# Graph network and mixture layers on one core: the last columns of the dense attention by heads, one-hots shared out by thirds, and the end of the edge layer

## The reference, cut to what matters

```python
e = jax.nn.leaky_relu(el[src] + er[dst], NEG_SLOPE)
m = jax.ops.segment_max(e, dst, num_segments=N)
ex = jnp.exp(e - m[dst])
den = jax.ops.segment_sum(ex, dst, num_segments=N)
out = jax.ops.segment_sum((ex / den[dst])[:, :, None] * feat[src], dst, num_segments=N)
```

```python
sigma = jax.nn.sigmoid(out_src[src] + out_dst[dst])
h = Uh + segment_sum(Vh[src] * sigma, dst) / (segment_sum(sigma, dst) + 1e-06)
x = x + relu(layernorm(h) * gamma + beta)
H = gelu(layernorm(x) @ W1 + b1)
probs = softmax(H @ Wg + bg); assign = argmax(probs)
out = x + probs[assign] * (H @ Wd[assign] + bd[assign])
```

## Time and profile before

| | before |
|---|---|
| median of 3 runs | 3075.07 us (3072.62 to 3076.36) |
| the profiled execution | 3073.93 us, span 3072.3 us |
| busy, share of the span | PE 82%, DVE 78%, ACT 40%, POOL 42% |
| matmuls, weight loads | 17969, 17970 |
| moved by DMA | 373.59 MB, 122 GB/s |

### The profile page before, as it was taken

The page is one execution under the profiler, slowest core; times in us unless marked ns, Lnnn a source line. Parts: engine busy times, 40 slices in busy tenths (PEclk is TensorE's granted clock), DMA queues, the critical chain, the costliest instruction groups (busy, mean ns, idle before and its releaser), DMA issues. The chain is left out here.

```text
span 3072.3 us, 51402 instructions
## 1 busy us (share of the span) xinstructions
PE 2510.4 (82%) x17969; PEld 1244.1 (40%) x17970; DVE 2406.3 (78%) x5293; ACT 1229.1 (40%) x2435; POOL 1284.2 (42%) x1499
## 2 busy tenths in 40 slices
PE   5888879999987999995899766777776777777598
PEld 3555545333354333344566421333333333323365
DVE  6988889999977999988443757777777777777477
ACT  5888860000010000002222435666666666666421
POOL 1666640000000000000560677777777777775055
PEclk8999999999998999995999887888889888888799
DMA  4000000000013000004331578888888888887343
GB/s 122 10 10 10 10 18 34 15 15 15 5 32 50 15 15 28 5 2 119 91 108 61 169 239 242 245 260 255 248 259 257 254 260 255 252 255 244 126 147 105
DMA packets 235588, 373.59 MB, mean 122 GB/s; under 512 B 83273, under 2 KB 165390, under 8 KB 233513
## 3 DMA queue, kind: packets, MB, share of 16 engines
q0 software_dynamic: 75536, 238.14, 25.8%
q1 hardware_dynamic: 156569, 128.66, 14.1%
q10 hardware_dynamic: 3200, 3.21, 0.4%
HBM read 324.84 MB, written 50.04 MB: 122 GB/s over the span
## 5 line engine op out<-in xcount | busy, mean ns | idle before, releaser
L1089 DVE SCALAR_TENSOR_TENSOR dense_W<-layer_B,steep,cnt 128x512 f32<-128x512 f32 (+1 forms) x1400 | 834.3, 675 | 7.7 <-PE dense_p_o L1147 5.0
L1147 PE MATMUL dense_p_o<-dense_W,feat 128*32 128x512 f32 (+1 forms) x8400 | 821.3, 541 | 23.0 <-DVE dense_W L1089 23.0
L2437 POOL DMA_INDIRECT Wd<-tab_d,ixq x544 | 519.9, 956 | 170.0 <-issue 166.6
L1147 PEld LDWEIGHTS dense_p_o<-dense_W,feat 128*32 128x32 f32 x8400 | 303.0, 110 | 512.2 <-issue 395.3
L1552 POOL MEMSET edst<- 128x782 int32 x1 | 0.8, 751 | 944.2 <-POOLq L1190 944.2
L2615 PE MATMUL strips_p_sg<-strips_sv,strips_oh 128*32 128x512 f32 x2000 | 316.1, 709 | 95.1 <-DVE strips_sv L2480 94.8
L2603 PE MATMUL strips_p_b<-strips_wrs,strips_ohT 96*128 96x256 bf16 x1000 | 176.4, 306 | 220.7 <-DVE strips_ohT L2451 203.6
L727 POOL TENSOR_SCALAR mix_L<-mix_back,encode_lowT 128x128 bf16<-128x128 f32 x392 | 244.8, 642 | 140.5 <-PE mix_p_c L887 140.4
L2544 ACT ACTIVATE strips_p_s<-strips_tv 128x1024 f32<-128x1024 f32 (+1 forms) x250 | 225.2, 901 | 157.8 <-DVE strips_sv L2480 145.8
L1104 ACT COPY dense_part<-dense_p_o 128x512 f32<-128x512 f32 (+1 forms) x42 | 19.6, 540 | 669.8 <-PE dense_p_o L1147 669.8
L2437 POOL DMA_INDIRECT strips_G<-tab_d,ixq x240 | 230.1, 959 | 73.2 <-issue 72.5
(11 more groups left out here) (529 smaller groups left out, 3864.8 us busy)
## 6 DMA issues: line engine op xcount, KB each, us to landing
strips_row<-dlr_d SPq DMA_DIRECT2D x250, 96.0 KB
ew<-in_ew SPq DMA_DIRECT2D x16, 1024.0 KB, 5.6
layer_B<-rise_d SPq DMA_DIRECT2D x12, 1024.0 KB, 4.7
hx_d<-strips_hrow SPq DMA_DIRECT2D x24, 512.0 KB, 5.4
Wd<-tab_d,ixq POOLq DMA_INDIRECT x544, 4.3
Wd<-in_fWd SPq DMA_DIRECT2D x8, 1024.0 KB, 8.4
tab_d<-feat SPq DMA_DIRECT2D x50, 128.0 KB, 2.4
tab_d<-gated_in_rowg SPq DMA_DIRECT2D x25, 256.0 KB, 2.1
```

Source lines behind the costliest of these rows:

```text
L1089: o = nc.vector.scalar_tensor_tensor(out=out, in0=rise, scalar=C.steep[:, q * H + h:q * H + h + 1], in1=count, op0=ALU.max, op1=ALU.mult)
L1147: m = nc.tensor.matmul(p_o[c % 2][h * MT:(h + 1) * MT, a, 0:n], feat[:, q, h, lo:lo + MT], W[t % 3][:, h, 0:n], start=(q == 0), stop=(q == ...
L2437: gp.indirect_dma_start(out=G[n % RING][:, j, :], out_offset=None, in_=C.tab3[:, :], in_offset=bass.IndirectOffsetOnAxis(ap=index, axis=0) ...
```

## The change

Counting: of three groups of edges, ACT now makes `L` for the first (`g % 3 == 0`) and POOL for the other two; the waits are counted accordingly. ACT makes 66 groups in place of 98, POOL 130 in place of 98 (520 instructions at L727 in place of 392).

Dense attention: the chunk of 53 destinations is taken out of the loop. For each head, DVE makes the weights of all 25 source blocks in two instructions of 25 x 53 = 1325 elements (a `max` of two broadcast operands, then a product with `cnt`), into `B[1]` for head 0 and `W[0..2]` for the others. PE takes them as the stationary operand, 53 columns, and streams 65 columns of `feat`: 25 matmuls a head that give 53 destinations on the partitions, so nothing is transposed, and ACT copies the 53 x 260 result into `acc` once. The transposes of the chunk before it are put between the matmuls of head 0.

Edge layer: the last block's GELU goes into a ring buffer of its own (`hidden`), no longer waits for the block before to have left `HT`, and its step is moved ahead of several steps of that block. The row buffers of the last two blocks are others. The last block's two stores are counted on a semaphore that the first gather of `stage_dense` waits for; the other waits at the end of the stage stay, that of the last row but one on a semaphore of its own.

```diff
@@ stage_encode_count, POOL, ACT, PE
-                for g in range(1, CG, 2):
+                for g in range(CG):
+                    if g % 3 == 0:
+                        continue
...
-                    if g % 2:
+                    if g % 3:
                         return
                     i, p = divmod(g, CP)
-                    k = g // 2 % 2
-                    if g >= 4:
-                        act.wait_ge(s_L, g // 2 - 1)
+                    k = g // 3 % 2
+                    if g >= 6:
+                        act.wait_ge(s_L, g // 3 - 1)
...
-                    pe.wait_ge(s_Lp if g % 2 else s_L, (g // 2 + 1) * (ET if g % 2 else 1))
+                    pe.wait_ge(s_Lp if g % 3 else s_L, (g - g // 3) * ET if g % 3 else g // 3 + 1)
@@ stage_attend_dense
+        full, last = N // DC, N % DC
...
+        flat = [W[k][:, :, :].rearrange("p h d -> p (h d)") for k in range(3)]
+        ends = [t[:, 0:NB * last].rearrange("p (b d) -> p b d", d=last) for t in [B[1][:, :, :, :].rearrange("p b h d -> p (b h d)")] + flat]
...
-                    for c in range(NDC):
+                    for c in range(full):
...
+                    v.wait_ge(s_B[0], 16 * (full // 2))
+                    steep = C.steep[:, :].rearrange("p (b h) -> p h b", h=H)
+                    for h in range(H):
+                        if h:
+                            v.wait_ge(s_mm, full * NB - 3 + h)
+                        nc.vector.tensor_tensor(ends[h], B[0][:, 0, h, 0:last].unsqueeze(1).broadcast_to([P, NB, last]),
+                                                steep[:, h, :].unsqueeze(2).broadcast_to([P, NB, last]), ALU.max).then_inc(s_most, 1)
+                        v.wait_ge(s_most, h + 1)
+                        nc.vector.tensor_tensor(ends[h], ends[h], C.cnt[:, :, full * DC:N], ALU.mult).then_inc(s_end, 1)
...
+                    act.wait_ge(s_sums, 1)
+                    nc.scalar.copy(C.acc[0:last, (NB - 1) * H * HW:NB * H * HW], p_o[0][0:last, 0, 0:H * HW]).then_inc(s_rest, 1)
...
-                    for b in range(blocks(NDC - 1)):
-                        turn(NDC - 1, b)
+                    pe.wait_ge(s_part, (full - 1) * NQ)
+                    for h in range(H):
+                        pe.wait_ge(s_end, h + 1)
+                        for q in range(NB):
+                            m = nc.tensor.matmul(p_o[0][0:last, 0, h * HW:(h + 1) * HW], ends[h][:, q, :], feat[:, q, h, :], start=(q == 0), stop=(q == NB - 1))
+                            if h == 0 and 8 <= q < 8 + blocks(full - 1):
+                                turn(full - 1, q - 8)
+                    m.then_inc(s_sums, 1)
@@ stage_strips
-            return tv[0][:, :, :].rearrange("p h d -> p (h d)") if b == NB - 1 else hrow[:, :]
+            return G[NE + 1][:, :, :].rearrange("p h d -> p (h d)")[:, 0:F] if b == NB - 2 else C.hrow[:, :]
+
+        def hidden(b):
+            return G[NE][:, :, :].rearrange("p h d -> p (h d)") if b == NB - 1 else HT
...
-                         (last - 1, two), (last - 1, two + 1), (last - 1, two + 2), (last - 1, two + 3), (last - 1, two + 4), (last - 1, two + 5),
-                         (last, one + 9), (last, two), (last, two + 1), (last, two + 2), (last, two + 3), (last, two + 4), (last, two + 5)):
+                         (last - 1, two), (last - 1, two + 1), (last, one + 9), (last - 1, two + 2), (last - 1, two + 3), (last - 1, two + 4),
+                         (last, two), (last, two + 1), (last - 1, two + 5), (last, two + 2), (last, two + 3), (last, two + 4), (last, two + 5)):
...
-                            sp.dma_start(C.hx_d[n * P:(n + 1) * P, 0:F], rowed(n)).then_inc(s_hd, 16)
-                    sp.wait_ge(s_xd, 16 * NB)
-                    sp.wait_ge(s_hd, 16 * NB)
+                            sp.dma_start(C.hx_d[n * P:(n + 1) * P, 0:F], rowed(n)).then_inc(C.s_rows if n == NB - 1 else s_last2 if n == NB - 2 else s_hd, 16)
+                    sp.wait_ge(s_xd, 16 * (NB - 1))
+                    sp.wait_ge(s_hd, 16 * (NB - 2))
+                    sp.wait_ge(s_last2, 16)
@@ stage_dense, POOL
                 gp.wait_ge(s_where, 1)
+                gp.wait_ge(C.s_rows, 32)
```

More of the change, by code:

```diff
@@ L1051, in stage_attend_dense @@
         s_r = sem("s_r"); s_acc = sem("s_acc"); s_pad = sem("s_pad"); s_used = sem("s_used")
+        s_most = sem("s_most"); s_end = sem("s_end"); s_sums = sem("s_sums"); s_rest = sem("s_rest")
         feat = C.feat[:, :].rearrange("p (b h d) -> p b h d", h=H, d=HW)
+        full, last = N // DC, N % DC
+        assert 0 < last <= P and NB * last <= H * DC and full % 2 == 0
+        flat = [W[k][:, :, :].rearrange("p h d -> p (h d)") for k in range(3)]
+        ends = [t[:, 0:NB * last].rearrange("p (b d) -> p b d", d=last) for t in [B[1][:, :, :, :].rearrange("p b h d -> p (b h d)")] + flat]
         def width(c):
@@ L1116, in keep @@
                                 nc.scalar.copy(to[:, :, lo:hi], p_r[u % 2][0:rows, a, :].rearrange("p (h d) -> p h d", h=H)[:, :, MT - (hi - lo):MT]).then_inc(s_acc, 1)
-                    for c in range(NDC):
+                    for c in range(full):
                         take(c)
                         keep(c)
+                    act.wait_ge(s_pad, 1)
+                    act.wait_ge(s_sums, 1)
+                    nc.scalar.copy(C.acc[0:last, (NB - 1) * H * HW:NB * H * HW], p_o[0][0:last, 0, 0:H * HW]).then_inc(s_rest, 1)
             @block.tensor
@@ L2303, in stage_strips @@
         st = sb("st", [P, 6]); mv = sb("mv", [P, 2]); rstd = sb("rstd", [P, 1]); st2 = sb("st2", [P, 6]); mv2 = sb("mv2", [P, 2]); rstd2 = sb("rstd2", [P, 1])
-        xn = [sb(f"xn{k}", [P, D]) for k in range(2)]; xT = sb("xT", [P, KC * P]); HT = sb("HT", [P, F]); hrow = sb("hrow", [P, F])
+        xn = [sb(f"xn{k}", [P, D]) for k in range(2)]; xT = sb("xT", [P, KC * P]); HT = sb("HT", [P, F])
         p_b = ps("p_b", [P, H, D]); p_s = ps("p_s", [P, H, D])
@@ L2582, in tail @@
                             act.wait_ge(s_tr, 2 * b + 1)
-                            if 1 <= b < NB - 1:
-                                act.wait_ge(s_hd, 16 * b)
+                            if b >= 1 and b != NB - 2:
+                                act.wait_ge(s_hd, 16 * min(b, NB - 2))
                             nc.scalar.copy(rowed(b)[:, 0:512], ffn(b)[:, 0:512]).then_inc(s_hr, 1)
```

29 lines of the change are left out of this document (12 added, 17 removed).

## The result

| | before | after |
|---|---|---|
| median | 3073.85 us of 4 runs (3072.07 to 3076.36) | 3052.61 us of 4 runs (3049.53 to 3055.14) |
| ratio, with its 95% interval | | 0.9932 (0.9919 to 0.9944) |
| the profiled execution | 3073.93 us | 3051.91 us, span 3050.2 us |

The account below looks back on a forecast made before the run. Counting was taken as bound by a chain between engines, none at its limit, and the dense end as a serial stretch. -10.6 - 8.6 - 3.9 = -23.1 us gave 3051 to 3052 us, range 3039 to 3067.

Parts of the forecast that it names:

- each kind of block: Counting: blocks with `near` ahead of `mix_z`, ahead of `mix_xn`, or between `mix_z` halves take 14.6, 15.1, 15.35 us; before, 15.5.
- the first kind: Counting: a block with `near` ahead of `mix_z` only, saving 0.9 us, forecast at 14.6 us.
- Counting, -10.6: Counting stage: 0.48 us saved a block over 24 blocks, 11.6, less 1 for POOL slowing DVE; bounds +7 and -36.
- The contention of POOL with DVE, put at 1 us: Counting: POOL's added work slows DVE's compares, 0.04 us a block, 1 us in all; bound 0.3 a block, 7 us.
- The two rivals of a counting stage that gains nothing or all of DVE's 36 us: Counting: DVE takes back ACT's gain, 3062 us, chance 0.12; or all DVE idle time is gained, 3027 us, chance 0.06.
- The rival named it for the dense end: Dense end: narrow matmuls drop PE's clock from 2.4 to 1.2 GHz, a step is 0.12 us; 3072 us, chance 0.06.
- 0.15 saved: Counting: in a block with `near` between the halves of `mix_z`, `first` starts at 223.35 in place of 223.52.
- the rival: its threshold of 0.73: Counting: POOL becomes the bound; compares growing from 0.64 to above 0.73 us lose the stage's gain; 3121 at 0.84, chance 0.05.
- Dense end, DVE: End of dense attention: DVE instructions of 1.53 us, 3.15 a head; its work falls from 18.8 to 12.6 us.
- Dense end, PE: End of dense attention: steps of 0.06 us, PE last, `acc` 4.3 us earlier a layer, -8.6 for both.
- The rival of added-up weight loads: Dense end: weight loads do not run beside streaming, a step is 0.104 us; 3067 us, chance 0.11.
- Edge end, -3.9: Edge layer's end: GELU 1.9 us earlier, SP's wait ends at 2886.1 in place of 2890.04; bounds -2 and -5.

Follow-up runs that it names:

- `e_place`: The changed kernel with ACT making the groups with remainders 4, 6 and 7 by 8 and POOL the other five: ratio 0.9895 to the kernel before.
- `e_gap`: The changed kernel with ACT making the groups with remainders 1, 4 and 6 by 8, one `near` between the halves of `mix_z` per block: ratio 0.9963 to before.
- `e_pool34`: The changed kernel with POOL making three groups out of four and ACT the fourth: ratio 0.9895 to the kernel before.
- `e_spare32`: The kernel before, with POOL also making unread one-hots of 33 further groups, the changed kernel's POOL load; ACT as before: ratio 1.0001.
- `e_count`: The kernel before with only the counting part of the change, the sharing by thirds: ratio 0.9971 to the kernel before, -8.9 us.
- `e_spare`: The kernel before, with POOL also making unread one-hots of 65 further groups, 163 in all; ACT as before: ratio 1.0052, 16 us slower.
- the split by halves: Two runs of the kernel before with half the edge layer's change each: earlier GELU with new row buffers, ratio 0.9992; later waits for the last stores, 1.0002.

## Why the prediction was right, point by point

- **Which view to read.** The block's chain, and not the busy shares, gave each kind of block to 0.1 us: 14.65, 15.09 and 15.26 against 14.6, 15.1 and 15.35. `e_place` and `e_gap`, which differ only in place, confirm it, and so does `e_pool34`, where every block is of the first kind.
- **Counting, -10.6, measured -9.2.** From the fourth block on, 21 blocks took 314.5 us in place of 325.1: 10.6 saved, 0.50 a block against 0.48. Two errors elsewhere partly cancel, and that is luck. The contention of POOL with DVE, put at 1 us, was 0 in the blocks (`e_spare32`). The pair of blocks ahead of the fourth, which I took as saving like the others, took 32.22 us in place of 30.90, 1.3 longer. With the clock at 1.00 it takes 30.53, as in `e_count`, so the fall cost 1.7. The two rivals of a counting stage that gains nothing or all of DVE's 36 us are out for this placement; `e_place` shows that place alone can take 20 of the 36.
- **The clock.** The rival named it for the dense end, where it stayed at 1.00. It acted in the counting stage, at a place that I had seen only as "0.15 saved": the `near` between the halves of `mix_z` opens a pause of 1.2 us on PE. I had priced what waits for the second half, not what the pause itself does.
- **POOL.** 87% busy and never waited for, as forecast. The price of 0.64 us was too high, and with it the rival: its threshold of 0.73 was further off than I said. Its mechanism is real (`e_spare`).
- **Dense end, DVE.** 1.54 an instruction and 3.03 a head, against 1.53 and 3.15. The wait of a product for its `max` was right (starts 1.57 apart); what I had not seen is that the next head's `max`, which doesn't wait for it, starts 1.46 after the product ahead of it, while that still runs.
- **Dense end, PE.** A step of 0.057 against 0.06, PE last by 6 us, `acc` after 18.62 us against 18.4 to 18.7. The rival of added-up weight loads is refuted: it would have made a step 0.104. The rule of the Trainium skill behind it (TensorE: Matmul & The Clock Gate, "The mechanism"), that loads overlap only where the row group (the rows of the array that a matmul uses) differs, doesn't hold for these 53 weight columns either, as the 0.057 us shows. The same section also lets a load run ahead when it goes to a background weight buffer, which my prediction left out; no run here can show that buffer.
- **Edge end, -3.9.** 2.0 for the GELU, 0.5 on the way to the last row, 1.4 for SP's wait; the split by halves gives 2.1 and 1.5. The forecast had the last row 1.9 us earlier and 2.0 behind it; measured are 2.5 and 1.4, so the exact sum is in part luck.

## What to carry to other kernels

Give work to another engine by place, not by number: in a loop whose engines take turns, a task costs nothing where its engine waits anyway and its full length between two links of the chain, and a rule by remainder of the loop's period can put every one where it is free. Price a neighbour's instruction by its mean over the stage, not over one stretch. And where an edit opens a pause of a microsecond on PE, look at the granted clock of the blocks behind it, not only at the wait.
